# Experts by token halves, and the stages behind them interleaved: the tail of a two-layer transformer kernel

## The chip, the core and the metric

The kernel runs on one core of a Trainium2 chip. The metric is the device time of one execution in microseconds, as the median of several runs. Five engines work side by side, each through its own instruction list in order: PE (TensorE, matrix products), DVE (VectorE), ACT (ScalarE), POOL (GpSimd) and SP (SyncE, which issues transfers). An instruction may wait until a semaphore has reached a value; everything behind it on the same engine then waits as well.

## The reference

The input `x` holds B=8 sequences of S=32 tokens, 256 tokens in all, each with C=256 values. Six blocks are added to it one after the other. The change touches the last four:

```python
x = x + L0_xattn(layernorm(x), ctx)      # not touched
x = x + L0_attn(layernorm(x))            # state-space block, not touched
# experts: for each token the best 2 of 8, weighted by a softmax of their logits
for e in range(8):
    g = clip(silu(n @ Wg[e]), -7, 7)
    out += ((g * (n @ Wu[e])) @ Wd[e]) * w_e
# read: masked attention over 512 memory vectors of the same sequence
attn = softmax(where(mask, n @ memory.T / 16, -1e30)); x = x + attn @ memory
# rotary attention, 16 heads, 4 key heads, head size 16, over the 32 tokens of a sequence
x = x + softmax(rope(q) @ rope(k).T / 4) @ v @ Wo
# last block, inner size 688, its weights taken from a table of 16 values by index
x = x + (silu(n @ gate.T) * (n @ up.T)) @ down.T
```

`n` is each time the layer norm of the current `x`. All products are in fp32.

## The kernel before

The first two blocks fill most of the time; the change touches only the tail behind them: `tail_pe`, `tail_act`, `tail_dve`. Each of these functions writes one engine's list by hand, in the order in which the calls stand; nothing reorders them. The 256 tokens are split in halves A (j=0) and B (j=1) of 128 tokens (4 sequences) each, since attention never crosses a sequence.

**Experts.** `ITEMS` (line 962) lists the work items. Experts 0 to 5 are one item each for all 256 tokens; experts 6 and 7 are two items each, in the order (6,A), (7,A), (6,B), (7,B), so there are ten. For an item n, `gate_up(n)` on PE (line 1062) makes the two products, ACT takes the silu (`silu`, line 1286), DVE clips it and multiplies (`activate`, line 1458), PE multiplies with the third matrix (`down`, line 1087), and DVE adds the weighted result to `x` (`add_expert`, line 1468). A whole-token item splits weights and inputs into a high and a low part in the format fp32r, and makes 24 matmuls of 256 columns (lines 1081 to 1083); ACT makes the high part of the weights (`hi_of_experts`) and DVE the low one (`lo_of_experts`). A half item uses plain fp32 weights: 16 matmuls of 128 columns in the trace's count (line 1078). One fp32 matmul of the code shows as two in the trace and as one in the lists of instructions below. The function `term` and `leaf` between them build parts of the last block's weights.

**Behind the experts.** Per half: norm (`half_stats` and `half_normal` on DVE, with the logarithm and exponential of `half_rstd` on ACT between them), a transposition on PE (`turn_half`, line 1116) and a copy of it to `hT` (`read_half`, line 1492). This comes three times, k=3, 4, 5, ahead of the read, of the rotary block and of the last block. The read is `read_scores`, `masked_scores`, `read_maxima`, `read_exponentials`, `turn_probs`, `copy_probs`, `read_mix`, `add_read`. The rotary block is `rotary_inputs` (keys, queries and values), `rotate_keys`, `rotate_queries`, `rotary_scores`, `rotary_shift`, `rotary_exponentials`, `rotary_sums`, `rotary_weights`, `rotary_mix`, `turn_heads`, `rotary_out`, `add_rotary`. The last block is `ffn_in`, silu and product, `ffn_down`, and the sum. In the list of PE the halves alternate: A's stage, then B's same stage. `keep_clock(7, ...)` at lines 1217 and 1220 issues seven matmuls of constants whose result nobody reads.

ACT holds one table of functions at a time: `preload_act_table(ACT.Silu)` or `preload_act_table_set("natural_log_exp_and_others")` changes it. PSUM has eight banks; the dictionaries at lines 974 to 977 say which product goes where.

## Time and profile before

| what | value |
|---|---|
| median of 3 runs | 472.26 us |
| range of the 3 runs | 472.26 to 474.9 us |
| the profiled execution | 469.32 us |
| its span, first to last instruction | 467.8 us |
| mean granted clock of PE over the span | 0.985 |
| PE busy over the span | 430.2 us, 92% |
| DVE busy | 363.0 us, 78% |
| ACT busy | 258.0 us, 55% |
| last 58 us of the span | the stages behind the experts |

The profile is one execution. Its timeline gives for each engine the start and the duration of instructions, and in brackets how long the engine stood idle before and whose work released it. Its chain follows the work that ended last back from the end. Its windows give the busy time of each engine and the granted PE clock in a stretch. Busy PE is not PE at its peak, since matmuls overlap: the last matmul of a row ends 0.16 us after the engine could start the next.

### The profile page before, as it was taken

What the parts mean: (1) busy time and instruction counts of PE and PEld (TensorE: products, weight loads), DVE (VectorE), ACT (ScalarE), POOL (GpSimd) and SP (SyncE); (2) the same over time, 40 slices, a digit from 0 to 9 for tenths busy, and PEclk for the clock granted to TensorE, in tenths of its full rate; (3) what the DMA queues carried; (4) which work ended last, traced back from release to release, by engine and by line L of the source; (5) the groups of instructions that cost most, each with busy time, mean ns of one, the idle gap of its engine ahead of it and who ended that gap; (6) DMA issues with size and microseconds to landing.
All of it is one profiled execution on the core that took longest, in us unless ns stands there. A gap on an engine that the chain in (4) does not pass through costs nothing.

```text
span 467.8 us, 6904 instructions
## 1 busy us (share of the span) xinstructions
PE 430.2 (92%) x2430; PEld 300.3 (64%) x2430; DVE 363.0 (78%) x761; ACT 258.0 (55%) x806; POOL 26.4 (6%) x33
## 2 busy tenths in 40 slices
PE   5987999979999999999999999998997899888597
PEld 2442444667887675767667775876584799736386
DVE  5888685849799869699799988976868798657631
ACT  1465889997553777766987586582113371231120
POOL 0000000000120000100001010100100021000000
PEclk9999999999999999999999999999989899999889
DMA  8267020314201105683645733893639679130000
GB/s 313 94 234 306 0 90 1 115 67 168 81 0 46 46 10 144 129 300 73 155 113 106 185 76 68 192 308 129 135 80 332 240 260 238 34 114 2 1 1 22
DMA packets 14047, 58.57 MB, mean 125 GB/s; under 512 B 1792, under 2 KB 2496, under 8 KB 12480
## 3 DMA queue, kind: packets, MB, share of 16 engines
q1 hardware_dynamic: 10992, 41.66, 24.0%
q0 software_dynamic: 3024, 16.52, 18.0%
q8 instruction: 17, 0.28, 0.2%
q14 instruction: 14, 0.11, 0.1%
HBM read 41.40 MB, written 0.26 MB: 89 GB/s over the span
## 4 chain that ended last, share of the span: by engine, by line
PE 73%; DVE 13%; ACT 11%; issue 2%; DMA 1%; DVEq 0%; ACTq 0%
PE PS L458 12%; PE PS L431 9%; PE PS L433 9%; PE PS L432 9%; PE PS L1713 3%; PE PS L478 3%; PE PS L1096 3%; ACT raw_dt.float L1845 3%; PE PS L1232 3%; PE PS L1742 2%; PE PS L505 2%; ACT raw_dt.float L1825 2%; PE PS L1078 2%; PE PS L467 1%; PE PS L1081 1%
## 5 line engine op out<-in xcount | busy, mean ns | idle before, releaser
L578 ACT ACTIVATE sq_dt.float<-PS 128x128 bf16<-128x128 f32 x256 | 67.1, 280 | 29.0 <-PE PS L433 22.2
L458 PE MATMUL PS<-s_dt.float,ctx_ring_dt.float 128*128 128x512 f32 x128 | 57.7, 593 | 1.3 <-DVE px_dt.float L812 1.3
L431 PE MATMUL PS<-wkc_dt.float32r,ctx_hi_dt.float32r 128*128 128x512 f32 x128 | 53.6, 419 | 1.5 <-ACT sq_dt.float L578 1.2
L578 ACT ACTIVATION_READ_ACCUMULATOR sq_dt.float<-PS 128x1 f32 x256 | 53.7, 211 | 0.0
L433 PE MATMUL PS<-wkc_dt.float32r,ctxT_ring_dt.float32r 128*128 128x512 f32 x128 | 50.2, 392 | 0.0
L432 PE MATMUL PS<-wkT_dt.float32r,ctx_hi_dt.float32r 128*128 128x512 f32 x128 | 50.2, 392 | 0.0
L1713 PE MATMUL PS<-wch_dt.float,xs_dt.float 128*128 128x512 f32 x96 | 42.2, 594 | 0.7 <-DVE xs_dt.float L1948 0.7
L458 PEld LDWEIGHTS PS<-s_dt.float,ctx_ring_dt.float 128*128 128x128 f32 x128 | 23.6, 190 | 25.0 <-issue 23.0
L655 ACT ACTIVATE luttmp_dt.float<-low_bit_dt.float,vec_dt.float,small_dt.float 128x1536 f32<-128x1536 uint8 x24 | 38.5, 1654 | 2.0 <-DMA lutw_dt.float<-luttmp_dt.float 2.0
L662 DVE SCALAR_TENSOR_TENSOR luttmp_dt.float<-idx_dt.float,luttmp_dt.float 128x1536 f32<-128x1536 uint8 x21 | 36.4, 1751 | 0.0
L431 PEld LDWEIGHTS PS<-wkc_dt.float32r,ctx_hi_dt.float32r 128*128 128x128 f32 x128 | 24.0, 187 | 14.0 <-ACT sq_dt.float L578 8.7
L1713 PEld LDWEIGHTS PS<-wch_dt.float,xs_dt.float 128*128 128x128 f32 x96 | 17.8, 190 | 22.3 <-issue 20.3
L668 POOL DMA_DIRECT2D lutw_dt.float<-luttmp_dt.float x21 | 18.3, 869 | 209.1 <-DVE luttmp_dt.float L662 209.1
L433 PEld LDWEIGHTS PS<-wkc_dt.float32r,ctxT_ring_dt.float32r 128*128 128x128 f32 x128 | 24.0, 188 | 5.6
L432 PEld LDWEIGHTS PS<-wkT_dt.float32r,ctx_hi_dt.float32r 128*128 128x128 f32 x128 | 24.1, 188 | 3.5
L799 DVE TENSOR_TENSOR s_dt.float<-s_dt.float,PS 128x2048 f32<-128x2048 f32 x8 | 18.3, 2287 | 10.3 <-PE PS L448 10.3
L431 PE MATMUL PS<-A_hi_dt.float32r,ctx_hi_dt.float32r 128*128 128x512 f32 x64 | 25.4, 396 | 0.0
L432 PE MATMUL PS<-A_dt.float32r,ctx_hi_dt.float32r 128*128 128x512 f32 (+1 forms) x64 | 24.9, 390 | 0.0
L433 PE MATMUL PS<-A_hi_dt.float32r,ctxT_ring_dt.float32r 128*128 128x512 f32 x64 | 24.9, 389 | 0.0
L695 DVE TENSOR_TENSOR s_dt.float<-PS,small_dt.float 128x512 f32<-128x512 f32 x32 | 21.6, 690 | 1.9 <-PE PS L433 0.9
L366 PE MATMUL PS<-consts_dt.float 128*128 128x512 bf16 x58 | 15.3, 416 | 5.0 <-DMA consts_dt.float<-in_consts 5.0
L561 ACT ACTIVATE A_hi_dt.float32r<-A_dt.float 128x1024 fp32r<-128x1024 f32 x8 | 8.4, 1054 | 18.9 <-PE PS L433 18.9
(294 smaller groups left out, 882.3 us busy)
## 6 DMA issues: line engine op xcount, KB each, us to landing
lutw_dt.float<-luttmp_dt.float POOLq DMA_DIRECT2D x21, 768.0 KB, 6.4
wch_dt.float<-in_chunks SPq DMA_DIRECT2D x6, 1024.0 KB, 4.9
ctxT_ring_dt.float<-in_ctxT SPq DMA_DIRECT2D x8, 512.0 KB, 3.9
ctx_ring_dt.float<-in_ctx SPq DMA_DIRECT2D x8, 512.0 KB, 3.4
keysT_dt.float<-in_ctxT SPq DMA_DIRECT2D x8, 512.0 KB, 7.8
keys_dt.float<-in_ctx SPq DMA_DIRECT2D x8, 512.0 KB, 7.5
luttmp_dt.float<-in_idx SPq DMA_DIRECT2D x3, 768.0 KB, 5.8
zu_dt.float<-in_wproj SPq DMA_DIRECT2D x1, 2048.0 KB, 7.3
```

The costliest lines, as they stand in the source:

```text
L366: nc.tensor.matmul(bank(nb), busy[:, 0:128], busy, start=True, stop=True)
L431: nc.tensor.matmul(o, x_hi, hi[:, c, :], start=c == 0, stop=False)
L432: nc.tensor.matmul(o, x_hi, lo[:, c, :], start=False, stop=False)
L433: last = nc.tensor.matmul(o, x_lo, hi[:, c, :], start=False, stop=c == CT - 1)
L458: last = nc.tensor.matmul(bank(5 + c), keysr[k][:, t, c * 128:c * 128 + 128], sS[k][:, t, :], start=t == 0, stop=t == KT - 1)
L578: last = nc.scalar.activation(sq[:, (4 * hf + g) * D:(4 * hf + g + 1) * D], bank(hf)[:, g * D:(g + 1) * D], ACT.Square, accum_out=ssq[:, k ...
L655: nc.scalar.activation(lutt[:, m, :], low_bit[:, m, :], ACT.Identity, scale=lut_gap[:, k:k + 1], bias=col("lut", 2 * k)).then_inc(lut_leaf, 1)
L662: nc.vector.scalar_tensor_tensor(lutt[:, m, :] if k else lutw[:, m, :], idx[:, m, :], float(2 * k), lutt[:, m, :], ALU.is_equal, ALU.mult) ...
L668: pool.dma_start(lutw[:, m, :], lutt[:, m, :], accum_op=ALU.add).then_inc(lut_added[m], 16)
L695: nc.vector.tensor_tensor(sS[k][:, t, :].rearrange("p (g q) -> p g q", g=G), score_bank(b, t, G, 64), krs[:, k, t, :].unsqueeze(2).broadca ...
L799: nc.vector.tensor_tensor(sS[k], sS[k], bank(4).unsqueeze(1).broadcast_to([128, KT, 512]), ALU.subtract)\
L1713: last = nc.tensor.matmul(bank(q), xs[:, VARIANT[n], c, j * 128:j * 128 + 128], wch[n % 2][:, c, hf * 512:hf * 512 + 512], start=c == 0, s ...
```

## The change

It alters the hand-written order of three engines, and the form of two experts. Experts 4 to 7 are now all half items: four items of A first, then four of B, twelve in all. On PE, ACT and DVE the calls of the later stages are laid out anew: items (6,B) and (7,B) stand among A's norm and scores, A's mix ahead of B's scores, B's read mix between A's rotary inputs and scores, A's rotary mix and output behind B's rotary inputs, A's first products of the last block ahead of B's rotary mix, A's `ffn_down` ahead of B's last norm. Banks, semaphores and the place of `probs` in SBUF follow from that. Both `keep_clock` calls are gone. ACT changes its table seven times in the tail where it did three times; `hi_of_experts` and `lo_of_experts` for experts 4 and 5 are gone. The diff, cut to its core:

```diff
-        ITEMS = [(e, (0, 1)) for e in range(NE - 2)] + [(e, (j,)) for j in range(TT) for e in (NE - 2, NE - 1)]
+        ITEMS = [(e, (0, 1)) for e in range(4)] + [(e, (j,)) for j in range(TT) for e in range(4, NE)]
...
         # tail_pe
-            for n in range(2, 7):
+            for n in range(2, 10):
                 gate_up(n)
                 down(n - 1)
-            gate_up(7)
-            gate_up(8)
-            down(6)
-            gate_up(9)
-            down(7)
-            down(8)
-            down(9)
...
+            gate_up(10)
             turn_half(3, 0)
+            down(9)
+            gate_up(11)
             read_scores(0)
+            down(10)
+            down(11)
+            turn_probs(0)
+            read_mix(0)
             turn_half(3, 1)
             read_scores(1)
-            turn_probs(0)
-            read_mix(0)
-            turn_probs(1)
-            read_mix(1)
+            turn_half(4, 0)
...
             rotary_inputs(0)
+            rotary_values(0)
+            turn_probs(1)
+            read_mix(1)
+            rotary_scores(0)
             turn_half(4, 1)
-            rotary_scores(0)
             rotary_inputs(1)
+            rotary_mix(0)
+            rotary_values(1)
+            rotary_out(0)
             rotary_scores(1)
-            keep_clock(7, 1)
-            rotary_mix(0)
-            rotary_out(0)
-            keep_clock(7, 2)
-            rotary_mix(1)
...
             turn_half(5, 0)
-            rotary_out(1)
-            ffn_in(0)
-            turn_half(5, 1)
-            ffn_in(1)
+            ffn_in(0, 0)
+            rotary_mix(1)
+            ffn_in(0, 1)
+            rotary_out(1)
             ffn_down(0)
+            turn_half(5, 1)
+            ffn_in(1, 0)
+            ffn_in(1, 1)
             ffn_down(1)
...
         # tail_act
             for n in range(len(ITEMS)):
                 silu(n)
-                if n + 2 < NE - 2:
+                if n + 2 < 4:
                     hi_of_experts(n + 2)
+                if n == 8:
+                    nc.scalar.preload_act_table_set("natural_log_exp_and_others")
+                    half_rstd(3, 0)
+                    nc.scalar.preload_act_table(ACT.Silu)
...
         # tail_dve
+            experts_done(0)
+            half_stats(3, 0)
             activate(9)
-            add_expert(7)
-            half_stats(3, 0)
             add_expert(8)
             half_normal(3, 0)
+            activate(10)
             add_expert(9)
             read_half(3, 0)
-            half_stats(3, 1)
-            half_normal(3, 1)
+            activate(11)
+            add_expert(10)
+            masked_scores(0)
+            read_maxima(0)
+            add_expert(11)
+            experts_done(1)
+            half_stats(3, 1)
...
```

**ACT, behind the silus of the experts.** L1291 is the silu of an item (moe from PSUM), L1304 and L1305 (afterwards L1295 and L1296) the logarithm and exponential of a norm, L1300 of the changed list the exponential of the read. Before:

```order
L1291 ACTIVATE moe_dt.float<-PS 128x512 [waits act_ready,gu_full] x2
L1291 ACTIVATE moe_dt.float<-PS 128x2x128 [waits act_ready,gu_full] x4
L1300 ACT_TABLE_LOAD
L1304 ACTIVATE small_dt.float<-small_dt.float 128x1 [waits ln_var]
L1305 ACTIVATE small_dt.float<-small_dt.float 128x1 [waits act_step]
L1304 ACTIVATE small_dt.float<-small_dt.float 128x1 [waits ln_var]
L1305 ACTIVATE small_dt.float<-small_dt.float 128x1 [waits act_step]
```

With the change:

```order
L1291 ACTIVATE moe_dt.float<-PS 128x2x128 [waits act_ready,gu_full] x5
L1330 ACT_TABLE_LOAD
L1295 ACTIVATE small_dt.float<-small_dt.float 128x1 [waits ln_var]
L1296 ACTIVATE small_dt.float<-small_dt.float 128x1 [waits act_step]
L1332 ACT_TABLE_LOAD
L1291 ACTIVATE moe_dt.float<-PS 128x2x128 [waits act_ready,gu_full] x3
L1333 ACT_TABLE_LOAD
L1300 ACTIVATE probs_dt.float,small_dt.float<-probs_dt.float,small_dt.float 128x512 [waits sc_shift]
```

A's first norm now lies between two table changes, ahead of the silus of the last three items, where it stood behind all of them.

**PE, from B's read mix on.** L1142 (L1135) is the read mix, L1119 (L1112) the transposition of a normed half, L1164 and L1169 (L1160 and L1165) rotary keys and queries, L1173 values, L1184 rotary scores, L1196 the rotary mix. Before:

```order
L1142 MATMUL PS<-keys_dt.float,probs_dt.float 32x256 [waits pt_ready_act]
L1142 MATMUL PS<-keys_dt.float,probs_dt.float 32x256 x15
L1119 MATMUL PS<-consts_dt.float,h_dt.float 128x128 [waits ln_done]
L1119 MATMUL PS<-consts_dt.float,h_dt.float 128x128
L1164 MATMUL PS<-hT_dt.float,rot_dt.float 128x128 [waits hT_ready,ld_rot,sc_shift]
L1164 MATMUL PS<-hT_dt.float,rot_dt.float 128x128 x3
L1169 MATMUL PS<-hT_dt.float,rot_dt.float 128x128 x8
L1173 MATMUL PS<-rot_dt.float,hT_dt.float 128x256 x2
L1119 MATMUL PS<-consts_dt.float,h_dt.float 128x128 [waits ln_done]
L1119 MATMUL PS<-consts_dt.float,h_dt.float 128x128
L1184 MATMUL PS<-rotact_dt.float 32x128 [waits rot_ready]
```

With the change:

```order
L1135 MATMUL PS<-keys_dt.float,probs_dt.float 32x256 [waits pt_ready_act]
L1135 MATMUL PS<-keys_dt.float,probs_dt.float 32x256 x15
L1184 MATMUL PS<-rotact_dt.float 32x128 [waits v_ready,rot_ready]
L1184 MATMUL PS<-rotact_dt.float 32x128 x15
L1112 MATMUL PS<-consts_dt.float,h_dt.float 128x128 [waits ln_done]
L1112 MATMUL PS<-consts_dt.float,h_dt.float 128x128
L1160 MATMUL PS<-hT_dt.float,rot_dt.float 128x128 [waits hT_ready]
L1160 MATMUL PS<-hT_dt.float,rot_dt.float 128x128 x3
L1165 MATMUL PS<-hT_dt.float,rot_dt.float 128x128 x8
L1196 MATMUL PS<-probs_dt.float,rotact_dt.float 32x64 [waits rp_ready]
```

Rotary inputs of A stood between B's read mix and the transposition of B; now the read mix comes behind them, and only A's scores (L1184) lie between it and the transposition, which waits for `ln_done`.

**DVE, from the sum of B's read on.** L1542 (L1549) is `add_read(1)`; L1481, L1482 and L1484 (L1491, L1492, L1494) are the statistics; L265 to L267 and L1489 (L1499) `half_normal`; L1575 to L1577 with the change are `rotary_shift(0)`. Before:

```order
L1542 SCALAR_TENSOR_TENSOR x_dt.float<-PS,small_dt.float,x_dt.float 128x256 [waits read_full]
L1481 BN_STATS small_dt.float<-x_dt.float 128x6 [waits x_ready]
L1482 BN_AGGR small_dt.float<-small_dt.float 128x2 [waits dve_step]
L1484 TENSOR_SCALAR small_dt.float<-small_dt.float 128x1 [waits ln_var]
L265 TENSOR_TENSOR small_dt.float<-small_dt.float 128x1 [waits ln_rstd,dve_step]
L266 SCALAR_TENSOR_TENSOR small_dt.float<-small_dt.float 128x1 [waits dve_step]
L267 SCALAR_TENSOR_TENSOR small_dt.float<-small_dt.float 128x1 [waits dve_step]
L1489 TENSOR_SCALAR h_dt.float<-x_dt.float,small_dt.float 128x256 [waits dve_step]
L1566 TENSOR_TENSOR rotact_dt.float<-PS,consts_dt.float 128x128 [waits qkv_full]
L1567 TENSOR_TENSOR rotact_dt.float<-PS,consts_dt.float 128x128
L1568 TENSOR_TENSOR rotact_dt.float<-rotact_dt.float 128x128 [waits dve_step]
L1494 COPY hT_dt.float<-PS 128x2x128 [waits turned]
```

With the change:

```order
L1549 SCALAR_TENSOR_TENSOR x_dt.float<-PS,small_dt.float,x_dt.float 128x256 [waits read_full]
L1491 BN_STATS small_dt.float<-x_dt.float 128x6 [waits x_ready]
L1492 BN_AGGR small_dt.float<-small_dt.float 128x2 [waits dve_step]
L1494 TENSOR_SCALAR small_dt.float<-small_dt.float 128x1 [waits ln_var]
L1575 STREAM_TRANSPOSE probs_dt.float<-PS 128x512 [waits rsc_full,dve_step]
L1576 TENSOR_REDUCE small_dt.float<-probs_dt.float 128x16 [waits dve_step]
L1577 TENSOR_TENSOR probs_dt.float<-probs_dt.float,small_dt.float 128x512 [waits dve_step]
L265 TENSOR_TENSOR small_dt.float<-small_dt.float 128x1 [waits ln_rstd]
L266 SCALAR_TENSOR_TENSOR small_dt.float<-small_dt.float 128x1 [waits dve_step]
L267 SCALAR_TENSOR_TENSOR small_dt.float<-small_dt.float 128x1 [waits dve_step]
L1499 TENSOR_SCALAR h_dt.float<-x_dt.float,small_dt.float 128x256 [waits dve_step]
L1504 COPY hT_dt.float<-PS 128x2x128 [waits turned]
```

`rotary_shift(0)`, three instructions over 512 columns, now stands between the statistics of B's norm and the scaling that gives PE its next operand.

## Rows read from the trace of the kernel before

**Rows 1.** The page: the chain that ended last, its shares of the span by engine.
```profile
PE 73%; DVE 13%; ACT 11%; issue 2%; DMA 1%; DVEq 0%; ACTq 0%
```

**Rows 2.** Timeline of PE, experts: start us, us, engine, line, op, out<-in, count.
```profile
388.10 1.89 PE L1096 MATMUL PS<-down_dt.float,moe_dt.float 128*128 128x256 f32 x8
...
392.65 1.89 PE L1096 MATMUL PS<-down_dt.float,moe_dt.float 128*128 128x256 f32 x8
394.37 1.95 PE L1078 MATMUL PS<-hT_dt.float,gu_b_dt.float 128*128 128x128 f32 x16
...
401.46 1.03 PE L1096 MATMUL PS<-down_dt.float,moe_dt.float 128*128 128x256 f32 x4
```

**Rows 3.** Timeline of PE, the stages behind the experts; in brackets idle before, releaser.
```profile
408.13 0.44 PE L1119 MATMUL PS<-consts_dt.float,h_dt.float 128*128 128x128 f32 x2 [1.22 <-DVE h_dt.float L1489]
...
412.37 1.92 PE L1127 MATMUL PS<-keysT_dt.float,hT_dt.float 128*32 128x512 f32 x16 [0.63 <-DVE hT_dt.float L1494]
...
415.65 1.93 PE L1142 MATMUL PS<-keys_dt.float,probs_dt.float 128*32 128x256 f32 x32 [0.78 <-ACT probs_dt.float L1314]
...
421.77 1.13 PE L1164 MATMUL PS<-hT_dt.float,rot_dt.float 128*128 128x128 f32 x8 [0.61 <-DVE hT_dt.float L1494]
...
427.53 1.16 PE L1164 MATMUL PS<-hT_dt.float,rot_dt.float 128*128 128x128 f32 x8
...
437.01 1.13 PE L1205 MATMUL PS<-rot_dt.float,probs_dt.float 128*128 128x256 f32 x4 [2.03 <-ACT probs_dt.float L1328]
...
443.00 1.47 PE L1197 MATMUL PS<-probs_dt.float,rotact_dt.float 32*32 32x64 f32 x64 [3.35 <-DVE probs_dt.float L1598]
...
446.99 6.39 PE L1232 MATMUL PS<-hT_dt.float,lutw_dt.float 128*128 128x128 f32 x48
...
459.59 5.35 PE L1240 MATMUL PS<-lutw_dt.float,ffn_dt.float 128*128 128x256 f32 x24
```

**Rows 4.** Timeline of DVE: product and sum of an item, norm of a half, softmax shift, last sum.
```profile
404.36 0.42 DVE L1465 TENSOR_TENSOR moe_dt.float<-moe_dt.float,PS 128x256 f32<-128x256 f32 x1 [0.24 <-PE PS L1078]
405.18 0.48 DVE L1475 SCALAR_TENSOR_TENSOR x_dt.float<-PS,small_dt.float,x_dt.float 128x256 f32<-128x256 f32 x1 [0.39 <-PE PS L1096]
...
408.95 0.42 DVE L1481 BATCH_NORM_STATS2 small_dt.float<-x_dt.float 128x6 f32<-128x256 f32 x1
...
409.62 0.15 DVE L1484 TENSOR_SCALAR small_dt.float<-small_dt.float 128x1 f32<-128x1 f32 x1
410.25 0.16 DVE L265 TENSOR_TENSOR small_dt.float<-small_dt.float 128x1 f32<-128x1 f32 x1 [0.48 <-ACT small_dt.float L1305]
...
410.83 0.41 DVE L1489 TENSOR_SCALAR h_dt.float<-x_dt.float,small_dt.float 128x256 f32<-128x256 f32 x1
...
427.77 0.72 DVE L1583 STREAM_TRANSPOSE probs_dt.float<-PS 128x512 f32<-128x512 f32 x1 [0.74 <-PE PS L1184]
...
429.24 0.69 DVE L1585 TENSOR_TENSOR probs_dt.float<-probs_dt.float,small_dt.float 128x512 f32<-128x512 f32 x1
...
464.97 0.42 DVE L1634 TENSOR_TENSOR x_dt.float<-x_dt.float,PS 128x256 f32<-128x256 f32 x1 [2.17 <-PE PS L1240]
```

**Rows 5.** Timeline of ACT: silu of an item, table load, exponential, copy of the probabilities.
```profile
403.41 0.38 ACT L1291 ACTIVATE moe_dt.float<-PS 128x256 f32<-128x256 f32 x1 [2.27 <-PE PS L1078]
403.81 1.28 ACT L1300 ACT_TABLE_LOAD   x1
...
412.94 0.72 ACT L1309 ACTIVATE probs_dt.float<-probs_dt.float,small_dt.float 128x512 f32<-128x512 f32 x1 [2.79 <-DVE small_dt.float L1533]
...
414.91 0.60 ACT L1314 ACTIVATE probs_dt.float<-PS 128x512 f32<-128x512 f32 x1 [1.16 <-PE PS L1134]
```

**Rows 6.** Windows: busy PE, PEld, DVE, ACT, POOL; granted clock, DMA share, GB/s.
```profile
366.00:371.00 5.00, 4.67 (x28) 4.58 (x28) 4.16 (x16) 0.32 (x2) 0.00 (x0) 0.66 0.51 203
435.00:437.00 2.00, 0.00 (x0) 0.00 (x0) 0.82 (x2) 1.07 (x5) 0.00 (x0) 1.00 0.03 8
441.00:449.00 8.00, 5.96 (x81) 5.06 (x82) 3.39 (x9) 1.14 (x7) 0.00 (x0) 0.57 0.01 2
```

More of the change, by code:

```diff
@@ L1165, in rotary_inputs @@
                                                 start=c == 0, stop=c == CT - 1)
-                last.then_inc(qkv_full, 1)
+                last.then_inc(kq_full, 1)
                 for a in range(4):
@@ L1500, in tail_dve @@
             add_expert(0)
-            for n in range(2, 7):
+            for n in range(2, 9):
                 activate(n)
-                if n + 2 < NE - 2:
-                    lo_of_experts(n + 2)
                 add_expert(n - 1)
```

182 lines of the change are left out of this document (92 added, 90 removed).

## The prediction

> **What bounds the kernel now.** I read the chain first: PE carries 73% of the time that ends last, DVE 13%, ACT 11%, DMA 1% [rows 1], so transfers are no term. Then the timeline of PE, since the change lays out its list anew. It has two parts. In the experts PE never waits: the reader is to see that each row begins where the one before ends [rows 2]. Behind them a bracket stands at nearly every row: PE waits for the norm, the softmax or a copy of the half that comes next [rows 3]. There the lists of DVE and ACT decide, and one instruction in front of the wrong one delays PE. The timelines of DVE and ACT give the lengths [rows 4, 5], the windows the clock [rows 6].
>
> **Experts.** An expert as one item costs one period, 392.65 - 388.10 = 4.55 us [rows 2]. A half item costs 1.79 for its gate and up products (1.95, less the 0.16 by which a last matmul outlives its issue) and 0.87 for the third (1.03 less 0.16) [rows 2], together 2.66; two make 5.32. For experts 4 and 5 that is 2 x 0.77 = +1.5 us on PE. What goes on ACT and DVE (the splitting of their weights) lay beside PE and gives nothing. The list `term` of DVE and the reduction of the mask stay where PE has slack.
>
> **The new order, leg by leg.** I carry one clock through the lists, each wait lasting until its last releaser. The third product of item 3 begins in both kernels' order after item 4's first one; item 4 starts at 388.10 - (4.55 - 1.72) = 385.3. Each leg ends where a row of before has the same operation.
>
> 1. To A's last expert sum: five times 1.79, one whole third product of 1.72, four halves of 0.87: 14.15, so 399.4, result at 399.6. The sum takes 0.48, the statistics and ACT's part of the norm 1.30 (408.95 to 410.25; DVE itself is free after 0.82, at 409.77) [rows 4]: 401.4. ACT now loads a table, 1.28, before it may take silu 9, 0.38 [rows 5]: 403.1. DVE's list has product 9 in front of the scaling: clip and product end 0.99 after the silu (403.79 to 404.78), then sum 8, 0.48, then the scaling, 0.99 (410.25 to 411.24) [rows 4]. PE transposes A at 405.5, before 408.13: 2.6 us early, after a wait of 1.7.
> 2. To A's read mix. Transposition 0.3, `down(9)` 0.87, `gate_up(11)` 1.79 bring A's scores to 408.4; they take 1.9 [rows 3]. But DVE's list has the sum of item 10 first: `down(10)` ends at 411.3, sum 0.48, mask and maximum 0.7 each (as the 512-column operations of DVE [rows 4]), exponential 0.72 with its accumulator 0.8 [rows 5], transposition 0.5 and the 0.78 that PE waited for its copy [rows 3]: 415.5 with some hand-overs. Before 415.65: the lead is spent.
> 3. To A's rotary inputs. Mix 2.1, sum and DVE's statistics 1.35, transposed norm copied to `hT` 0.4 (a 256-column operation like the product [rows 4]) with 0.15 to PE: B's scores start at 419.6, before 412.37. Scores 1.95, mask and maximum 1.4, only then the copy of A's next norm, 0.4: 423.5, before 421.77, 1.7 late.
> 4. To B's rotary inputs. Keys are 8, queries 16 matmuls of 128 columns, at 1.79 / 16 = 0.112 each [rows 2] 2.7, values 0.87 as a half third product; transposition and copy of the probabilities 1.3; B's mix 2.1; sum and statistics 1.35: 431.9. Here DVE runs `rotary_shift(0)`, 427.77 to 429.93 in before, 2.16 [rows 4], and then the scaling 0.99: PE, idle since 430.8, transposes B at 435.1 and starts its inputs at 436.1, before 427.53: 8.6 late.
> 5. To A's rotary output: inputs 2.7 without values, mix 1.0 (1.47 at the low clock [rows 3], so between 0.74 and that), values 0.87: 440.8, before 437.01, 3.8 late. The old kernel waited 2.03 there [rows 3].
> 6. To A's last block: output 1.13, sum and statistics 1.35, `rotary_shift(1)` 2.16 again ahead of the scaling 0.99, transposition and copy 1.0: 447.5, before 446.99, 0.5 late. PE idles from 442.2 to 446.4.
> 7. To the end. A's first products 48 x 0.112 = 5.4, B's mix 1.0 and output 0.97, `ffn_down` 2.6 (half of 5.35 [rows 3]), what B's norm outlasts it by with transposition and copy 1.4, B's products 5.4, `ffn_down` 2.8: 19.6, so the last sum starts at 467.1. The row is 464.97 [rows 4]: +2.1. Before needed only 17.98 from 446.99, although A's products ran in 6.39 there [rows 3], 0.8 more than 5.4 and 0.16.
>
> The removed 14 matmuls of `keep_clock` stood in waits and give nothing by themselves. The four added table loads: one is in leg 1; those at B's last norm fit into PE's `ffn_down`. The loads of the rotary weights are issued at B's last expert sum, about 413.8, and are wanted at 423.5; if they took longer than these 9.7 us, leg 4 would grow by the rest.
>
> The Trainium skill, "ScalarE: Activation LUTs", section "What ACT_TABLE_LOAD costs", says that each change to another table costs the load, about 1.28 us, plus a drain of about 1.38. The row shows 1.28, begun 0.02 after the silu's end [rows 5], so I take no drain. By the page's rule leg 1 would be 1.4 longer and the sum with it.
>
> **The clock.** Between 441 and 449 PE's granted clock was 0.57 on average, so it stood at 1.2 instead of 2.4 GHz for (1 - 0.57) x 2 x 8 = 6.9 us; between 366 and 371, 0.66, for 3.4 us [rows 6]. The first fall came in the idle 3.35 us before 443.00 [rows 3], the second among short work and waits. An idle stretch of 2.0 us at 435 left the clock at full [rows 6]. The new order has two idle stretches, 4.3 and 4.2 us, each followed by a short transposition and another 0.7 us wait. I expect both to bring the clock down. What one costs: half of the busy time at the low clock, 3.4 / 2 = 1.7 to (6.9 - 1.0) / 2 = 2.9. I take 2.1, nearer the shorter, since PE then has dense work. Nothing hides it: matrix products follow on the chain both times. 2 x 2.1 = 4.2.
>
> The Trainium skill, "TensorE: Matmul & The Clock Gate", section "What's actually happening", says that "the default state is throttled, and activity releases the throttle"; the trace agrees, and by it dropping `keep_clock` speaks against the change.
>
> **Sum.** +2.1 + 4.2 = +6.3 us: the span 467.8 becomes 474.1, the profiled execution 469.32 becomes 475.6. The median of before lies 2.94 above its profiled execution; carried over, 472.26 + 6.3 = 478.6. A measurement tells about 1% of it, 4.7 us.
>
> **Rivals.**
> - The clock stays up (0.24). If at least one of the two idle stretches leaves it at full, because the short operations in them count, the change is worth +2.1 to +4.2: 474.4 to 476.5. For: 2.0 us idle did nothing. Against: 3.35 us did. Not slower by the bound.
> - The clock also falls in A's read (0.10). PE idles 2.2 us, transposes, idles 0.8 more, about 411.7 to 415.2. Priced at half of the 2 us mix and half of the 1.9 us scores, +1 to +2: 479.6 to 480.6. The drain of the table page gives 1.4 more too, about 480.0.
> - The halves cover each other (0.06). If what DVE has in front of a norm is ready early and the waits of 1.7, 2.2, 1.8, 4.3 and 4.2 us, some 14, come out at half, the change wins: 478.6 - 7 - 4.2 = 467.4. It is one mechanism: DVE must reach the two `half_normal` calls of legs 4 and 6 without the shift in front; it decides if their wait on PE is under 2.5 us. Against: the lists say what stands in front, and the shift depends on scores of the same half that PE makes just before.
>
> **How the numbers follow.** The forecast has 0.56 (477 to 480.5), the rivals 0.24, 0.10 and 0.06; 0.04 is for a saving between the second and the last. Leg sums may err by 1 us, the two clock terms by 0.8 each. The range 471.5 to 481.5 cuts half of the winning case and the far end of the slow one. Slower by over 1% (above 477.0): the third case and most of the forecast, 0.63. Within 1%: the first rival and the low end of the forecast, 0.30. Faster by over 1%: 0.07.
>
> **What would show it.** Right: the brackets at PE's transpositions. The one ahead of B's rotary inputs names DVE's h and over 3.5 us, as does that ahead of A's last block; the first one at some 405.5; A's read mix near 415.5; a clock of 0.5 in the windows after both. Wrong: PE's idle behind the experts no larger than before, or a clock at 1.00 up to the end. If the last sum starts before 463 the leg reckoning fails, not the clock.

## The result, and the profile after

| | before | after |
|---|---|---|
| median of 4 runs each, same chip | 473.58 us | 480.67 us |
| range of the 4 runs | 472.26 to 475.28 | 477.3 to 482.63 |
| profiled execution, its span | 469.32, 467.8 | 482.63, 481.1 |
| mean granted clock of PE | 0.985 | 0.965 |
| PE, DVE, ACT busy | 430.2, 363.0, 258.0 | 438.2, 361.5, 261.6 |

The change makes the kernel slower by 7.1 us: ratio 1.0163, 95% interval 1.0117 to 1.0209. The prediction had +6.3 us and a median of 478.6; the kernel before took 473.58 here, 1.3 above the 472.26 that the prediction started from.

To keep the unchanged front of the program out of the reading, I measure a **stretch**: from the start of item 4's first product on PE to the start of the last sum on DVE. It was 385.27 to 464.97 in the kernel before, 79.70 us (the start is 394.37 less two periods of 4.55 [rows 2]; the end [rows 4]). In the changed kernel it is 389.14 to 478.32, 89.18 us: +9.5. The other 3.9 us of the two profiled executions lie in front, in code that is the same in both; the section on the reasons comes back to that, and it is one reason why this profile, the slowest of the four runs, shows more than the medians.

PE's timeline of the changed kernel, experts and what follows; columns are start us, duration us, engine, line, operation, out<-in, count, and in brackets idle before and releaser:

```profile
403.26 1.95 PE L1078 MATMUL PS<-hT_dt.float,gu_a_dt.float 128*128 128x128 f32 x16
...
405.91 1.95 PE L1078 MATMUL PS<-hT_dt.float,gu_b_dt.float 128*128 128x128 f32 x16
409.21 0.44 PE L1112 MATMUL PS<-consts_dt.float,h_dt.float 128*128 128x128 f32 x2 [1.35 <-DVE h_dt.float L1499]
...
417.96 0.66 PE L1127 MATMUL PS<-consts_dt.float,probs_dt.float 128*128 128x128 f32 x4 [1.88 <-ACT probs_dt.float L1300]
419.39 2.85 PE L1135 MATMUL PS<-keys_dt.float,probs_dt.float 128*32 128x256 f32 x32 [0.78 <-ACT probs_dt.float L1305]
...
424.15 3.35 PE L1120 MATMUL PS<-keysT_dt.float,hT_dt.float 128*32 128x512 f32 x16 [1.29 <-DVE hT_dt.float L1504]
...
429.47 1.13 PE L1160 MATMUL PS<-hT_dt.float,rot_dt.float 128*128 128x128 f32 x8 [1.60 <-DVE hT_dt.float L1504]
...
440.89 0.69 PE L1112 MATMUL PS<-consts_dt.float,h_dt.float 128*128 128x128 f32 x2 [4.13 <-DVE h_dt.float L1499]
442.09 2.08 PE L1160 MATMUL PS<-hT_dt.float,rot_dt.float 128*128 128x128 f32 x8 [0.52 <-DVE hT_dt.float L1504]
443.96 3.62 PE L1165 MATMUL PS<-hT_dt.float,rot_dt.float 128*128 128x128 f32 x16
...
449.46 1.03 PE L1204 MATMUL PS<-rot_dt.float,probs_dt.float 128*128 128x256 f32 x4
...
454.97 0.69 PE L1112 MATMUL PS<-consts_dt.float,h_dt.float 128*128 128x128 f32 x2 [4.05 <-DVE h_dt.float L1499]
456.27 6.17 PE L1230 MATMUL PS<-hT_dt.float,lutw_dt.float 128*128 128x128 f32 x32 [0.61 <-DVE hT_dt.float L1504]
```

The rows at 403.26 and 405.91 are two half items one behind the other: a period of 2.65 us, the 2.66 of the prediction. Then the reader is to see the brackets: 1.35 us ahead of A's transposition, 1.88 ahead of A's probabilities, 4.13 ahead of B's transposition, 4.05 ahead of A's last one. And the durations: B's read scores take 3.35 us where the same row took 1.92 before [rows 3]; the keys 2.08 where 1.13 stood; the queries 3.62 for 1.95; 32 products of the last block 6.17.

The two long brackets name DVE's h. DVE's timeline around the first of them:

```profile
437.57 0.15 DVE L1494 TENSOR_SCALAR small_dt.float<-small_dt.float 128x1 f32<-128x1 f32 x1
437.76 0.72 DVE L1575 STREAM_TRANSPOSE probs_dt.float<-PS 128x512 f32<-128x512 f32 x1
438.51 0.69 DVE L1576 TENSOR_REDUCE small_dt.float<-probs_dt.float 128x16 f32<-128x512 f32 x1
439.23 0.69 DVE L1577 TENSOR_TENSOR probs_dt.float<-probs_dt.float,small_dt.float 128x512 f32<-128x512 f32 x1
...
440.42 0.41 DVE L1499 TENSOR_SCALAR h_dt.float<-x_dt.float,small_dt.float 128x256 f32<-128x256 f32 x1
```

The statistics of B's norm end at 437.72; the softmax shift of A's rotary scores (three rows, 437.76 to 439.84) stands ahead of the scaling at 440.42, as leg 4 said. At 451.85 to 454.50 the same pattern stands for leg 6. Ahead of A's probabilities it is PE's turn to be late: the sum of item 10 waits for `down(10)`, and A's mask (415.65) stands behind it:

```profile
415.25 0.48 DVE L1485 SCALAR_TENSOR_TENSOR x_dt.float<-PS,small_dt.float,x_dt.float 128x256 f32<-128x256 f32 x1 [2.44 <-PE PS L1096]
415.65 0.68 DVE L1537 SCALAR_TENSOR_TENSOR probs_dt.float<-PS,mask_dt.float 128x512 f32<-128x512 f32 x1
```

Windows of the changed kernel (busy PE, PEld, DVE, ACT, POOL, then the granted clock, DMA share, GB/s):

```profile
48.00:55.00 7.00, 5.94 (x7) 2.52 (x8) 5.16 (x25) 4.07 (x8) 0.00 (x0) 0.51 0.00 0
420.00:427.00 7.00, 5.71 (x45) 1.84 (x34) 3.20 (x12) 0.50 (x2) 0.00 (x0) 0.52 0.34 121
428.00:440.00 12.00, 6.60 (x96) 5.04 (x96) 6.60 (x20) 2.33 (x7) 0.00 (x0) 1.00 0.01 2
441.00:447.00 6.00, 5.48 (x25) 5.08 (x26) 3.34 (x8) 0.00 (x0) 0.00 (x0) 0.50 0.00 0
448.00:454.00 6.00, 2.92 (x73) 2.07 (x69) 3.77 (x11) 1.44 (x7) 0.00 (x0) 1.00 0.01 3
455.00:461.00 6.00, 5.39 (x24) 5.02 (x25) 2.67 (x5) 1.57 (x2) 0.00 (x0) 0.50 0.00 0
```

Behind the experts lie three stretches at 1.2 GHz, one behind each wait, and between them the clock is back at 2.4. The first row is one in front, in unchanged code.

### The profile page after: what moved, and what is told of

Its sections match the earlier page's. It is cut to its first block, busy times and chain, and to the rows that moved or that the text cites. A ratio compares the mean times of both kernels' runs of the same rounds, so it can differ in the third digit from the quotient of the medians.

```text
span 481.1 us, 6917 instructions
## 1 busy us (share of the span) xinstructions
PE 438.2 (91%) x2430; PEld 305.7 (64%) x2432; DVE 361.5 (75%) x763; ACT 261.6 (54%) x810; POOL 26.3 (5%) x33
## 4 chain that ended last, share of the span: by engine, by line
PE 74%; DVE 11%; ACT 11%; issue 2%; DMA 1%; SPq 0%; DVEq 0%; ACTq 0%
PE PS L458 11%; PE PS L431 9%; PE PS L433 8%; PE PS L432 8%; PE PS L1756 3%; PE PS L1727 3%; PE PS L478 3%; PE PS L1230 3%; PE PS L1096 3%; ACT raw_dt.float L1859 3%; PE PS L505 2%; PE PS L1078 2%; ACT raw_dt.float L1839 2%; PE PS L467 1%; PE PS L366 1%
## 5 line engine op out<-in xcount | busy, mean ns | idle before, releaser
L1756 PE MATMUL PS<-zu_dt.float,wkc_dt.float 128*128 128x512 f32 x32 | 17.5, 702 | 3.5 <-ACT beta_dt.float L1825 3.5
```

Of the source, the lines that this page charges most:

```text
L1756: nc.tensor.matmul(bank(ring(f"A{n}", i)), wkc[:, 4 * n + g, c * 128:c * 128 + 128], uT[:, 2 * g:2 * g + 2, :], start=True, stop=True).the ...
```

## The experiments

Every kernel was timed in rounds beside the kernel before; its median is given with that of before on the same chip, and the ratio with its 95% interval. `keep_clock(n, b)` is the kernel's own filler: n products of 512 bf16 columns into bank b, some 0.22 us each, with no use for the result. The runs of one kernel spread over 4 to 7 us, so where an edit is worth less, its verdict rests on the stretch. The stretch is read from one profiled execution of each kernel, and falls of the clock differ between executions; so stretches are compared only with the falls in them named.

**Is it the clock? Fillers in the three waits (`a_fill`).**

```diff
             down(11)
+            keep_clock(8, 3)
             turn_probs(0)
...
             rotary_scores(0)
+            keep_clock(18, 7)
             turn_half(4, 1)
...
+            keep_clock(18, 7)
             turn_half(5, 0)
```

> The changed kernel with dummy matmuls (8, 18 and 18 of 512 columns) put into three idle stretches of PE: ahead of the transposition of A's read probabilities, of B's ahead of the rotary inputs and of A's ahead of the last block. Nothing else moves. Call the tail the time from PE's first matmul of item 4 to the start of the last sum: 79.7 us before, 89.2 with the change. Theory 1 (three falls of the clock cost 7.2 of the +9.5, the order 2.1): the clock stays at 1.00 behind the experts, the tail is 81.5 to 82.5, the median falls by 5 to 8 us to about the kernel before or 1% above. Rival (the order itself costs most, the clock is only a sign of idle): clock up, tail still above 86, median down by less than 3.

Median 475.84 beside 473.97, ratio 1.0042 (1.001 to 1.0074). The stretch went from 89.18 to 81.43 us (390.82 to 472.25) at full clock:

```profile
389.00:473.00 84.00, 74.99 (x715) 58.36 (x713) 48.15 (x130) 22.59 (x49) 2.62 (x3) 1.00 0.24 59
```

PE's rows have the durations of a fast clock again, and the waits are as long as they were (a row of fillers, 4.06 us, stands in each long one). So 7.75 of the 9.5 us are the clock, and 1.7 are the order against the kernel before with the fall that it had itself:

```profile
421.08 1.93 PE L1135 MATMUL PS<-keys_dt.float,probs_dt.float 128*32 128x256 f32 x32 [0.78 <-ACT probs_dt.float L1308]
...
428.82 1.13 PE L1161 MATMUL PS<-hT_dt.float,rot_dt.float 128*128 128x128 f32 x8 [1.59 <-DVE hT_dt.float L1507]
...
436.04 4.06 PE L366 MATMUL PS<-consts_dt.float 128*128 128x512 bf16 x18
440.23 0.44 PE L1112 MATMUL PS<-consts_dt.float,h_dt.float 128*128 128x128 f32 x2
...
446.00 1.03 PE L1205 MATMUL PS<-rot_dt.float,probs_dt.float 128*128 128x256 f32 x4
```

The medians say less: +7.1 us became +1.9, so there the fillers are worth 5.2. The profiled execution of the changed kernel had a mean clock of 0.965, its three other runs 0.975, so in those the clock was low for less time.

**Only the two long waits filled (`a_fill_late`).** As above without the first `keep_clock(8, 3)`.

> The changed kernel with fillers (18 products each) only in the two long waits ahead of PE's transpositions of B's second norm and A's last norm; the wait in A's read, about 411.7 to 415.2 in my reckoning, is left as it was. Stretch meant: from the start of item 4's products on PE to the last sum; it took 89.18 us in the changed kernel, 81.43 with all three waits filled. Theory (each fall of the clock stands by itself, the one in A's read is worth what the two others are, 2.1 to 2.9 us): the granted clock falls once, around A's read mix, the stretch takes 83.5 to 84.3 us, time about 2.4 us above the kernel with all three filled. Rival (the fall in A's read is paid by waits of PE on DVE behind it, so it costs nothing): the clock falls there as well, but the stretch takes 81.4 to 82.0 us. Second rival: the clock stays up in the whole stretch, the fall in A's read was a consequence of the others' times: 81.4 us.

Median 474.67 beside 473.45, ratio 1.0062 (1.0031 to 1.0094). The stretch is 82.92 us, 1.49 over `a_fill`. The clock fell once, for 3.4 us, on A's read mix (3.44 us for 1.93), and stood at full from 421 to the end:

```profile
417.68 3.44 PE L1135 MATMUL PS<-keys_dt.float,probs_dt.float 128*32 128x256 f32 x32 [0.78 <-ACT probs_dt.float L1307]
...
417.00:421.00 4.00, 3.32 (x32) 1.57 (x32) 1.00 (x5) 0.92 (x3) 0.00 (x0) 0.57 0.93 310
```

In this profile the fall in A's read stands by itself, against both rivals, but it was shorter and cheaper than I expected (1.5, not 2.1 to 2.9). In the changed kernel the fall at the same place lasted 6.8 us.

**The order, leg 6: A's last norm ahead of B's shift (`a_norm_first`).** On the changed kernel, without fillers:

```diff
-            rotary_shift(1)
             half_normal(5, 0)
             read_half(5, 0)
+            rotary_shift(1)
...
             ffn_in(0, 0)
-            rotary_mix(1)
             ffn_in(0, 1)
+            rotary_mix(1)
```

(B's shift also reads its scores in four pieces, so that PE may write other banks beside it.)

> The changed kernel with DVE taking A's norm and its copy ahead of the rotary shift of B (leg 6), the shift's transposition in four pieces, and PE taking both parts of A's last-block products ahead of B's rotary mix. Theory 1 (the shift in DVE's list in front of the norm delays PE by its 2.16 us): the wait of PE ahead of A's transposition falls from 4.05 to about 1.9, the tail by 1.5 to 2.2 from the order, and by up to 2.5 more if the clock then stays up: 85 to 87.7. Rival (DVE's two halves are serial work, the shift is only late instead): PE's wait moves to B's mix, the tail stays within 0.7 of 89.2 at the same falls of the clock.

Median 478.37 beside 473.97, ratio 1.013 (1.0068 to 1.0191). PE's wait ahead of A's last transposition fell to 2.42 us:

```profile
444.04 1.03 PE L1204 MATMUL PS<-rot_dt.float,probs_dt.float 128*128 128x256 f32 x4
...
447.92 0.44 PE L1112 MATMUL PS<-consts_dt.float,h_dt.float 128*128 128x128 f32 x2 [2.42 <-DVE h_dt.float L1499]
```

From A's rotary output to A's transposition it is 447.92 - 444.04 = 3.88 us against 454.97 - 449.46 = 5.51. The shift's place costs 1.6 us there. But the clock fell behind this wait too (448 to 453), and it had fallen behind the two others, which this kernel leaves as they were. The stretch is 86.45 us (384.48 to 470.93), 2.7 less than in the changed kernel: 1.6 are this wait, the rest came with shorter falls, 3.4 us in place of 6.8 in the read and behind this wait. The profiled execution is the fastest of its four.

**Leg 4 in the same way (`a_fill_norm41`).** On `a_fill`, with 8 fillers instead of 18 and the shift of both halves in four pieces:

```diff
-            rotary_shift(0)
             half_normal(4, 1)
             read_half(4, 1)
+            rotary_shift(0)
```

> The changed kernel with all three waits filled, with B's second norm (scaling and copy) put ahead of A's rotary softmax shift on DVE, the shift's transposition in four pieces, and 8 fillers instead of 18 ahead of PE's transposition of B. It tests the third rival of the prediction, that DVE has to reach this norm without the shift in front of it. My theory of the lists (DVE carries both halves one after the other, what is taken out in front of B's norm comes in front of A's exponentials): PE's transposition of B comes 2.1 us earlier, A's rotary mix about as late as before or later, and the stretch to the last sum takes 81.4 to 82.4 us, no gain. Rival (the wait for the shift is the cost of leg 4): it falls by most of 2.16 us, to 79.3 to 79.8 us.

Median 478.19 beside 472.29, ratio 1.0163 (1.0109 to 1.0218). The stretch is 83.99 us (384.77 to 468.76), 2.6 longer, not shorter:

```profile
432.56 0.44 PE L1112 MATMUL PS<-consts_dt.float,h_dt.float 128*128 128x128 f32 x2 [0.67 <-DVE h_dt.float L1502]
...
438.92 1.27 PE L1197 MATMUL PS<-probs_dt.float,rotact_dt.float 32*32 32x64 f32 x64 [2.46 <-DVE probs_dt.float L1596]
440.11 2.07 PE L1173 MATMUL PS<-rot_dt.float,hT_dt.float 128*128 128x256 f32 x4
```

B is transposed 47.79 us after the start of the stretch instead of 49.41, but A's rotary mix begins at 54.15 instead of 53.24, after a new wait of 2.46 us, at whose end the clock falls once more (the values take 2.07 for 1.13; together with the mix and the output 1.5 us). What is left, some 1 us, is DVE's own list: taken from in front of B's norm, the shift is late for A. The exponential of ACT, which ran beside B's norm before, now has nothing beside it, and DVE waits for it:

```profile
436.42 0.69 DVE L1589 TENSOR_REDUCE small_dt.float<-probs_dt.float 128x16 f32<-128x512 f32 x1 [0.70 <-ACT probs_dt.float L1317]
```

With these 0.70 us and the transposition in four pieces, which takes 0.90 for 0.72, the 0.91 by which A's mix begins later is accounted for. The wait of leg 4 is not the price of leg 4. The profiled execution, 473.08, is by far the fastest of its five (the others took 477.9 to 479.3), so the stretch shows less than the median; what the slower ones lost was not seen.

**Leg 2: A's mask ahead of the sum of item 10 (`a_fill_mask`, `a_fill_mask2`).** On `a_fill`:

```diff
             activate(11)
-            add_expert(10)
...
             masked_scores(0)
             read_maxima(0)
+            add_expert(10)
             add_expert(11)
```

> The changed kernel with all three waits filled, and on DVE the masking and the maximum of A's scores put ahead of the sum of item 10. It tests leg 2 of the prediction, that this sum in front is what takes A's lead away. Theory: A's probabilities are ready earlier by the wait for down(10) and the sum, the stretch from item 4 to the last sum falls from 81.43 to about 80.0 us (-1.4). Rival (PE's third products of items 10 and 11 and their sums end late as well, and take the place): no change, 81.2 to 81.6 us.

Median 474.15 beside 473.45, ratio 1.003 (0.9992 to 1.0069), stretch 81.06: almost nothing. The mask did begin 1.45 us earlier, but my own 8 fillers kept PE busy beyond the probabilities. So the same with `keep_clock(2, 3)`:

> As a_fill_mask, but with 2 fillers instead of 8 in the first wait: in a_fill_mask the mask began 1.45 us earlier as meant (25.07 against 26.52 us after item 4's first products), yet the 8 fillers kept PE busy until 28.49 and the stretch to the last sum was 81.06 us. Theory (the fillers ate the gain, leg 2 is right): A's probabilities are transposed about 27.3 us after item 4's start, the clock stays at full, the stretch takes 80.0 to 80.3 us. Rival (the gain is lost again later in PE's order, whatever the fillers): 81.0 to 81.4 us. Second rival (with 2 fillers the clock falls in A's read): 82.0 us or more.

Median 473.14 beside 472.29, ratio 1.0025 (0.9983 to 1.0067). The stretch is 80.04 (388.19 to 468.23), 1.39 less than in `a_fill`: what leg 2 said stands in front of A's softmax was all of it.

```profile
413.28 0.69 DVE L1539 SCALAR_TENSOR_TENSOR probs_dt.float<-PS,mask_dt.float 128x512 f32<-128x512 f32 x1 [1.41 <-PE PS L1120]
...
417.03 1.93 PE L1135 MATMUL PS<-keys_dt.float,probs_dt.float 128*32 128x256 f32 x32 [0.78 <-ACT probs_dt.float L1308]
```

**The other side: the kernel before without its fillers, with more, and with fillers everywhere.** `b_nokeep` drops both `keep_clock(7, ..)`; `b_fill` has 22 in place of the second 7; `b_fill_all`:

```diff
+            keep_clock(5, 0)
             turn_half(3, 0)
...
+            keep_clock(2, 0)
             read_scores(0)
             turn_half(3, 1)
+            keep_clock(2, 0)
             read_scores(1)
             turn_probs(0)
+            keep_clock(3, 4)
...
             turn_probs(1)
+            keep_clock(3, 4)
             read_mix(1)
...
+            keep_clock(5, 4)
             rotary_scores(0)
...
-            keep_clock(7, 2)
+            keep_clock(21, 2)
             rotary_mix(1)
```

> The kernel before without its two calls of keep_clock. Theory 1 (they stand in waits, their only worth is the clock): same starts of PE's real work up to A's rotary output, the clock falls earlier, already in the idle stretch ahead of A's output or soon behind, and stays low longer: tail 79.7 becomes 80.5 to 82, median +0.5 to +3. Rival (worth nothing, since the clock falls in spite of them): tail within 0.4 of 79.7.

> The kernel before with 22 instead of 7 dummy matmuls ahead of B's rotary mix, which fill the wait of 3.35 us. Theory 1: the clock stays at 1.00 from 440 to 449, B's mix, transposition, output and A's products run 2.4 us faster in sum, tail 77.2 to 77.8, median -1.5 to -3, faster than both kernels. Rival (the fillers outlast the wait and push B's mix back, or the clock falls elsewhere in the tail): tail 79 to 81, no difference.

> The kernel before with fillers in every wait of PE behind the experts where a bank is free: 5 ahead of A's first transposition, 2 ahead of each half's scores, 3 ahead of each read mix, 5 ahead of A's rotary scores, 21 in place of 7 ahead of B's rotary mix. Theory (the clock falls only where PE idles or does short work): clock 1.00 from item 4 on, stretch to the last sum 77.3 to 77.8 us against 79.70 in the kernel before, time 2 to 3 us below the kernel before where that one's clock falls at the end. Rival (falls come at other places whatever is filled, as with 22 in one wait alone): low stretches of 3 to 7 us remain and the stretch takes 79.5 to 81.6 us.

| | median (before) | ratio | stretch | low clock in it |
|---|---|---|---|---|
| before | | | 79.70 | 441 to 449 |
| `b_nokeep` | 474.75 (473.97) | 1.0 (0.9956 to 1.0045) | 81.52 | 439 to 456 |
| `b_fill` | 472.22 (473.97) | 0.9985 (0.9941 to 1.0029) | 81.59 | 413 to 420, 443 to 448 |
| `b_fill_all` | 470.38 (473.45) | 0.996 (0.9911 to 1.0009) | 79.95 | 435 to 443 |

Without its fillers the old order had the clock low for 17 us and the stretch was 1.8 longer in the profiled execution, though the medians do not tell the two apart. With 22 fillers in one place (`b_fill`) it fell for 3.4 us at the end and, for 6.8 us, in the read, where B's scores took 3.64 us for 1.92:

```profile
416.17 3.64 PE L1127 MATMUL PS<-keysT_dt.float,hT_dt.float 128*32 128x512 f32 x16 [0.63 <-DVE hT_dt.float L1494]
```

The fall in the read is not the work of the edit. PE's list up to there is that of the kernel before, with the same waits ahead of the fall (1.22 and 0.61 us), and in the profile of before the clock stayed at full there. So one profile does not tell whether a fall comes at a place in every execution. With every wait filled that has a free bank (`b_fill_all`) it fell behind A's rotary mix, the one wait that has none:

```profile
433.32 1.02 PE L1202 MATMUL PS<-probs_dt.float,rotact_dt.float 32*32 32x64 f32 x64 [0.32 <-DVE probs_dt.float L1604]
436.37 2.08 PE L1210 MATMUL PS<-rot_dt.float,probs_dt.float 128*128 128x256 f32 x4 [2.03 <-ACT probs_dt.float L1334]
438.24 6.66 PE L366 MATMUL PS<-consts_dt.float 128*128 128x512 bf16 x21
444.83 1.04 PE L1202 MATMUL PS<-probs_dt.float,rotact_dt.float 32*32 32x64 f32 x64
...
435.00:443.00 8.00, 6.63 (x17) 3.14 (x18) 4.38 (x13) 1.57 (x7) 0.00 (x0) 0.57 0.00 0
```

The fall costs twice there: the output takes 2.08 for 1.13, and the 21 fillers, now slow themselves, run 6.66 us where the wait behind them was shorter. From the output to B's mix it is 8.46 us, in the kernel before 443.00 - 437.01 = 5.99 [rows 3], so 0.95 for the output and 1.5 for fillers that outlast the wait. Up to B's mix the kernel before took 57.73 us, from there to the last sum `b_fill_all` took 464.60 - 444.83 = 19.77: the old order at full clock is worth 77.50, an estimate from two runs that I could not reach in one. My expectations of 77.2 to 77.8 us for `b_fill` and `b_fill_all` missed; in both the rival came, falls at other places.

**One part of the change alone: experts 4 to 7 as halves, the rest in the old order (`b_fill_halves`).** `b_fill_all` with the items, their banks and their lists as in the changed kernel.

> As the kernel before with fillers in every wait, and of the change one part alone: experts 4 to 7 as twelve items (four whole, A's four, B's four), with the old order of everything behind the experts. Theory (leg 1: each of experts 4 and 5 as two halves takes 5.32 us of PE in place of 4.55): the stretch from item 4 to the last sum is 1.5 us longer than in the kernel with every wait filled, about 78.8 to 79.3 us, and PE never waits in the experts. Rival 1 (unsplit halves also free DVE and ACT of the splitting, which was not hidden): 0 to -1 us. Rival 2 (DVE, with twice as many products and sums of 256 columns, becomes the bound of the items): +2.5 us or more, and PE's rows in the experts show waits for DVE.

Median 472.11 beside 473.45, ratio 0.9985 (0.9944 to 1.0027). From item 4's first product to the first filler behind the last third product PE takes 413.60 - 390.67 = 22.93 us, in `b_fill_all` 406.12 - 384.65 = 21.47: +1.46, the 1.5 of the prediction, with no bracket between the items:

```profile
410.09 1.95 PE L1078 MATMUL PS<-hT_dt.float,gu_b_dt.float 128*128 128x128 f32 x16
411.87 1.89 PE L1096 MATMUL PS<-down_dt.float,moe_dt.float 128*128 128x256 f32 x8
413.60 1.24 PE L366 MATMUL PS<-consts_dt.float 128*128 128x512 bf16 x5
```

The whole stretch, 79.89, is as long as that of `b_fill_all` and not the 78.8 to 79.3 that I expected: the clock was low here as well, but for 3.4 us in place of 6.8 (443 to 447), and the fillers outlasted the wait by less.

**What the runs point to (`a_best`, `b_best`).** `a_best` is the changed kernel with fillers, A's mask and A's last norm in front (9 fillers in the wait ahead of A's last norm); `b_best` is `b_fill_all`. Both also have this, in an early wait of PE at 45 us and ahead of the experts:

```diff
+                    if n == 0 and i == 3:
+                        pe.wait_ge(proj_read, 9)
+                        keep_clock(9, 0)
                     nc.tensor.matmul(bank(ring(f"A{n}", i)), wkc
...
-            keep_clock(11, 6)
+            keep_clock(15, 6)
             turn_norm(2, (6, 3))
+            keep_clock(2, 5)
             pe.wait_ge(hT_ready, 2)
```

> The changed kernel with what the runs so far speak for: A's mask and maximum ahead of the sum of item 10, A's last norm ahead of B's rotary shift on DVE (its transposition in four pieces) and both of A's last-block product groups ahead of B's rotary mix on PE, fillers of 2, 18 and 9 in the three waits, 9 in the early wait at 45 us, 15 in place of 11 and 2 more ahead of the experts. Theory: stretch from item 4 to the last sum 79.0 to 79.6 us, no fall of the clock anywhere, time 468 to 470 us, clearly below both kernels. Rival (the front's low clock comes by chance and not from the wait at 44 to 48 us): low stretches at 47 to 55 us stay in some runs and the times have two groups as before, median about 473 us.

> The kernel before with fillers in every wait behind the experts (as b_fill_all), and 9 fillers in the early wait at 45 us, 15 in place of 11 and 2 more ahead of the experts. Theory: the fall of the clock at 47 to 55 us and that at 366 to 371 us go, each worth 1.5 to 3.4 us; the fall after A's rotary mix (64 small products, then 2.0 us of waiting, where no bank is free for a filler) stays; time 466 to 468 us, faster than both kernels. Rival (the early fall comes by chance): median about 470 us as in b_fill_all, in two groups 5 us apart.

Five rounds each, beside a before of 472.29: `a_best` 471.22, ratio 0.9981 (0.9946 to 1.0015), stretch 79.12; `b_best` 470.37, ratio 0.9982 (0.9949 to 1.0014), stretch 78.77. The times of 468 to 470 and 466 to 468 us that I expected were missed. Both beat the changed kernel; neither is shown to beat the kernel before. Their slowest runs are better (471.9 and 472.0 of 12 runs each, against 475.7 of 29); the mean clock was 0.993 or more in each of their 24 runs, and neither profile has the fall at 47 to 55 us. The fillers ahead of the experts won nothing: the clock stood at full from 366 to 371, where it was 0.66 [rows 6], and then PE stood for 2.16 us and waited for DVE's list of the routing. In `b_best`:

```profile
366.00:371.00 5.00, 4.67 (x39) 4.58 (x39) 3.98 (x15) 0.58 (x1) 0.00 (x0) 1.00 0.39 153
...
375.45 1.97 PE L1097 MATMUL PS<-down_dt.float,moe_dt.float 128*128 128x256 f32 x8 [2.16 <-DVE moe_dt.float L1472]
372.03 1.04 POOL L1367 CAST mask_dt.float<-maskraw_dt.float 128x1024 f32<-128x1024 uint8 x1 [30.17 <-PE PS L1084]
372.11 0.99 DVE L1461 TENSOR_TENSOR small_dt.float<-small_dt.float 128x16 f32<-128x16 f32 x1
...
373.17 1.05 POOL L1368 TENSOR_SCALAR mask_dt.float<-mask_dt.float 128x1024 f32<-128x1024 f32 x1
373.34 0.90 DVE L1463 TENSOR_TENSOR small_dt.float<-small_dt.float 128x16 f32<-128x16 f32 x1
```

The rows point to why. POOL's cast of the mask waits for PE's products (`<-PE`), so faster products release it earlier: at 372.03, where the kernel before has it at 373.18. It now lies beside the small products of DVE's routing, and two of them take 0.99 and 0.90 us where the same rows took 0.17 and 0.18 before. They end when POOL's rows end, in `a_best` as in `b_best`. So the gain of the clock was lost: from the start of the product ahead of the fillers (L1048) to that of item 4 it is 26.3 us in `b_best` and 25.6 in the kernel before. That POOL is what held DVE is read from these rows, and spans on POOL are rough; no run moved the cast away to test it.

## Why the prediction was right

**The legs.** Every milestone of the reckoning, moved by the start of item 4 (385.3 there), can be held against both kernels. "At full clock" is `a_fill`, start 390.82, so +5.52; for the changed kernel, start 389.14, it is +3.84.

| milestone | reckoned | `a_fill`, less 5.52 | changed, less 3.84 |
|---|---|---|---|
| A transposed (leg 1) | 405.5 | 405.4 | 405.4 |
| A's read mix (2) | 415.5 | 415.6 | 415.6 |
| A's rotary inputs (3) | 423.5 | 423.3 | 425.6 |
| B transposed (4) | 435.1 | 434.7 | 437.1 |
| A's rotary output (5) | 440.8 | 440.5 | 445.6 |
| A's last products (6) | 447.5 | 447.0 | 452.4 |
| last sum (7) | 467.1 | 466.7 | 474.5 |

At full clock no milestone is off by more than 0.5 us. Reading the lists with durations of the old trace was enough to place every wait: who stands in front on DVE, when its input comes, which releaser is last. The sum of the order was +2.1 and came out at +1.7, against a kernel before whose own fall is in its 79.70. Against the old order at full clock (77.50) the new one is 3.9 longer: 1.46 for the halves and 2.5 for the stages behind them. Leg 2's claim was tested and held (1.39 us). Of the two shifts in front of a norm, which legs 4 and 6 have in common, only that of leg 6 could be moved with a gain. The loads of the rotary weights, which could have lengthened leg 4, did not: PE's bracket at A's rotary inputs names DVE (1.60 us).

**The table.** ACT's load of the Silu table ahead of silu 9 began 0.02 us after the exponential and the silu 0.01 after the load; no 1.38 us follow, so leg 1 holds without a drain, and the 480.0 that the sum would be with one is near the measured 480.67 by chance:

```profile
405.11 0.20 ACT L1296 ACTIVATE small_dt.float<-small_dt.float 128x1 f32<-128x1 f32 x1
405.33 1.28 ACT L1332 ACT_TABLE_LOAD   x1
406.62 0.76 ACT L1291 ACTIVATE moe_dt.float<-PS 128x256 f32<-128x256 f32 x2
```

**The clock, a mis-sized term.** The two falls came where they were expected, at the end of the two long waits. The term was 2 x 2.1 = 4.2. Measured, as differences to `a_fill` at the same milestones: in leg 4 and 5 5.14 - 2.33 = 2.81 us (A's output), in legs 6 and 7 7.75 - 5.14 = 2.61 us (last sum). The 2.1 was too close to the short one of the two falls of before: each of these lasted 6.8 us, and PE had dense products for most of it (2.08 and 3.62 us, then 6.17). The old order's own fall, 2.2 us by the reckoning above, was as long but cheaper: it began at 442, an idle microsecond ahead of B's mix [rows 3], and small products and a transposition lay in it.

**The fall in A's read came as well.** I gave the second rival 0.10. It costs 2.33 us by A's rotary inputs (0.92 in the mix, 1.43 in B's scores), where the rival said 1 to 2. I had held that the transpositions between the waits of 1.9 and 0.8 us would keep the clock up, as the 2.0 us at 435 had [rows 6]. They did not, in the one profile of each of the three kernels that left this wait open. The term should have been 7.75, not 4.2. By its mechanism this is the case of the second rival. The number does not decide between them: that rival had 479.6 to 480.6, the forecast itself 477 to 480.5, and the median is 480.67.

**Why the time still came out near.** +1.7 and +7.75 make +9.5 in the profiled execution, while the medians differ by 7.1. Against it I had +6.3. Of the 2.1 us between 478.6 and 480.67, 1.3 are the kernel before, whose median moved. The changed kernel's profile is its slowest run: the first projection starts 1.2 us later (16.54 for 15.35), and the clock's fall at 48 to 55 us makes it 4.1 by 58 us; what comes then nearly cancels. That fall is no work of the change: of four kernels with the old order and the same front three had it in their profile, though the kernel before itself did not. That its runs lie in groups, near 469.5, 472 and 474.5, may come in part from there (in its fastest group the mean clock was 0.982 to 0.989, in its slowest 0.971 to 0.982); it was not shown, since the runs of `a_best` still lie in two groups 2.5 us apart with the same mean clock. Part of the agreement is luck: a clock term that is 3.5 too small, and falls that do not all come, or not at full length, in every run (the fall in A's read took 3.4 us in two kernels and 6.8 in another).

**The rivals.** That the clock stays up is refuted by the profile. That the halves cover each other is too, for this order: the condition I set (PE's wait ahead of B's and A's norms under 2.5 us) was met in leg 6 (2.42 us) and nearly in leg 4 (some 2.5), each place by itself, and gave 1.6 us there and a loss here, far from the 11 that rival needed. With all that the runs point to, `a_best` (79.12) stands beside `b_best` (78.77), so the idea of two interleaved halves is not shown to lose by itself, and not to win. Taking the two `keep_clock` calls out of the old order lost 1.8 us of the stretch; in the new order their old places are gone, and what counts is whether the long waits hold dense work.

## What to carry to other kernels

Interleaving two halves by hand can pay only if the engine that serves both, here DVE, has room: carry one clock through its list, and look at what stands in front of each instruction that PE waits for. Then price every new wait twice, once as idle time and once as what the matrix products behind it lose at half the clock; here the new order cost 3.9 us at full clock and the products at half the clock 7.75 more. A filler helps only while it is shorter than the wait it stands in, and one that runs at the low clock takes twice as long, so it can push the end itself. An engine that gets faster also releases others earlier: look at what they will then lie beside. And if the runs of a kernel lie in groups, compare a stretch that holds the change, not the span.

## What the runs showed of the hardware that I had not expected

- The granted clock fell in or behind waits of 1.9 to 2.5 us: in A's read (`a_fill_late`, 1.88 and 0.78 us of idle with a transposition between them), at 64 small products (32 x 64) and 2.03 us (`b_fill_all`), behind 2.42 us (`a_norm_first`), behind 2.46 us with small products next (`a_fill_norm41`). The same 2.03 us had left it at full in the profile of before [rows 6], where it fell 5 us later, in the next wait.
- The same instructions with the same waits in front had the clock at full in one execution and low in another: B's read scores took 1.92 us in the kernel before and 3.64 in `b_fill`.
- Removing a fall may only move it: fillers ahead of the experts took that at 366 us away, and in `a_best` one came at 375, behind the 2.16 us in which PE now waited for DVE. In `b_best` the same wait had none behind it (the row took 1.97 us).
- Two products of DVE over 16 columns took 0.99 and 0.90 us in place of 0.17 and 0.18 with rows of POOL over 1024 columns beside them (`a_best`, `b_best`).
- The fall at 47 to 55 us, behind a wait of 3.54 us, came in some kernels and not in others, though their program is the same up to there; with 9 fillers in that wait it was in neither profile.
